# A recommendation tower on one core: ten tables looked up on TensorE in pairs, with loads of 112 + 13 partitions, rings for rows and pairs, and five parts

## The reference, cut to what matters

```python
e = jnp.stack([tbl_0[ids[:, 0]], ..., tbl_25[ids[:, 25]]], axis=1)      # 512 x 26 x 128
all_emb = jnp.concatenate([bottom_output[:, None, :], e], axis=1)       # 512 x 27 x 128
gram = jnp.einsum('bfd,bgd->bfg', all_emb, all_emb)
z = gram[:, _TRIU_I, _TRIU_J]                                           # 512 x 351
h = jnp.concatenate([z, r_bottom_output], axis=1)
h = jnp.maximum(h @ W_top1 + b_top1, 0.0)                               # 512 x 512
h = jnp.maximum(h @ W_top2 + b_top2, 0.0)                               # 512 x 256
y = h @ W_top3                                                          # 512 x 1
```

## Time and profile before

| | |
|---|---|
| three runs | 166.47, 171.18, 188.59 (median 171.18) |
| the profiled execution, from first to last instruction | 164.9 |
| TensorE busy with matmuls | 111.2 (67%), 700 records |
| GpSimd busy | 79.3 (48%), 72 gathers among it |
| VectorE, ScalarE busy | 60.0 (36%), 54.4 (33%) |
| HBM read, written | 13.70 MB, 1.49 MB |
| mean granted TensorE clock | 0.845 of full |

### The profile page before, as it was taken

How to read it: one execution, slowest core, us unless ns; L and a number is a source line. 1 busy time by engine, 2 the same in 40 slices (tenths; PEclk the granted TensorE clock), 3 DMA queues, 4 the chain that set the end, 5 groups by cost and what they waited for, 6 DMA issues and landing times.

```text
span 164.9 us, 1891 instructions
## 1 busy us (share of the span) xinstructions
PE 111.2 (67%) x700; PEld 97.8 (59%) x700; DVE 60.0 (36%) x109; ACT 54.4 (33%) x78; POOL 79.3 (48%) x81
## 2 busy tenths in 40 slices
PE   6809949968734968935300006259999999999784
PEld 6707737746624746925200006139999989979583
DVE  1046956965808494202000020042364442531110
ACT  3051963574627192202000020043354433342011
POOL 4277877887778787777777777100000000010200
PEclk9975896999997899996955555555899999999999
DMA  2954554566546942212212211106114152006100
GB/s 52 247 159 162 180 186 156 178 188 191 169 158 191 227 137 79 61 48 50 62 48 48 63 49 48 32 0 90 44 28 74 36 79 43 16 0 93 48 0 0
DMA packets 19501, 15.32 MB, mean 93 GB/s; under 512 B 13764, under 2 KB 15680, under 8 KB 19492
## 3 DMA queue, kind: packets, MB, share of 16 engines
q1 hardware_dynamic: 14562, 10.06, 22.3%
q0 software_dynamic: 2416, 4.82, 11.6%
q10 hardware_dynamic: 2514, 0.32, 1.3%
HBM read 13.70 MB, written 1.49 MB: 92 GB/s over the span
## 4 chain that ended last, share of the span: by engine, by line
PE 36%; DMA 30%; issue 18%; DVE 5%; ACT 4%; another core or an unknown queue 3%; SPq 2%; ACTq 1%; DVEq 0%
PE banks L460 19%; DMA lookup_ids_sb<-in_lookup_ids 14%; DMA raw<-in_tbl 13%; PE banks L498 5%; PE banks L441 4%; DVE low L646 3%; PE banks L505 3%; DMA products_dram<-products 2%; PE banks L424 2%; ACT products L598 2%; PE banks L426 2%; DVE one_hot L632 2%; ACTq L323 1%; DMA pairs<-products_dram 1%
## 5 line engine op out<-in xcount | busy, mean ns | idle before, releaser
L358 POOL DMA_INDIRECT mixed_sb<-in_mixed_table,mixed_rows_sb x64 | 67.8, 1059 | 22.1 <-issue 19.2
L460 PE MATMUL banks<-turned 128*112 128x104 f32 x256 | 34.1, 292 | 30.7 <-issue 25.3
L460 PEld LDWEIGHTS banks<-turned 128*112 128x112 f32 x256 | 31.8, 206 | 32.1 <-issue 30.6
L424 PE MATMUL banks<-one_hot,high 125*128 125x512 f32 x60 | 27.6, 459 | 16.7 <-DVE low L646 14.3
L598 DVE COPY products<-banks 112x416 f32<-112x416 f32 (+2 forms) x17 | 14.0, 839 | 57.3 <-PE banks L460 29.5
L598 ACT COPY products<-banks 112x416 f32<-112x416 f32 (+2 forms) x17 | 14.1, 843 | 57.7 <-PE banks L460 29.9
L632 DVE TENSOR_SCALAR one_hot<-lookup_ids_sb,starts_sb 125x512 fp32r<-125x512 int32 x60 | 26.6, 490 | 18.0 <-DMA lookup_ids_sb<-in_lookup_ids 12.8
L426 PE MATMUL banks<-one_hot,low 125*128 125x512 f32 x60 | 26.6, 444 | 0.0
L424 PEld LDWEIGHTS banks<-one_hot,high 125*128 125x128 f32 x60 | 13.4, 223 | 21.7 <-issue 18.5
L323 POOL DMA_DIRECT2D products_dram<-products x1 | 0.8, 846 | 44.0 <-DVE products L598 44.0
L683 ACT CAST high<-raw 125x1024 fp32r<-125x1024 f32 (+1 forms) x8 | 8.8, 1101 | 29.0 <-DMA raw<-in_tbl 29.0
(11 more groups left out here) (32 smaller groups left out, 75.1 us busy)
## 6 DMA issues: line engine op xcount, KB each, us to landing
raw<-in_tbl SPq DMA_DIRECT2D x6, 500.0 KB
lookup_ids_sb<-in_lookup_ids SPq DMA_DIRECT2D x8, 256.0 KB, 8.7
raw<-in_tbl SPq DMA_DIRECT2D x2, 625.0 KB
products_dram<-products SPq DMA_DIRECT2D x12, 91.0 KB
mixed_sb<-in_mixed_table,mixed_rows_sb POOLq DMA_INDIRECT x64
pairs<-products_dram SPq DMA_DIRECT2D x16, 39.0 KB
w_sb<-in_w SPq DMA_DIRECT2D x2, 256.0 KB
w_sb<-in_w SPq DMA_DIRECT2D x1, 512.0 KB
```

Of the source, the lines that this page charges most:

```text
L358: pool.indirect_dma_start(mixed_sb[:, n, :], None, mixed_table, bass.IndirectOffsetOnAxis(ap=mixed_rows_sb[:, n:n + 1], axis=0),).then_inc ...
L424: pe.matmul(lookup_ps[:, i % 2, :], high[0:TABLE_PARTS, i % 2, c, :], columns, start=(c == 0), stop=False)
L460: last = pe.matmul(product_ps[0:QUAD * SLOTS, b % 2, k // half, k % half, 0:QUAD * OTHERS], turned[:, t, q, :, :].rearrange("p j f -> p (j ...
```

## The change

- Ten tables are looked up on TensorE (six of 1,000 rows, four of 1,250), and no side gathers are left. The two tables join the lookups; the mixed table has the same 16 tables.
- Two tables of the same size form a duo. Their ids stand side by side, so that one instruction makes the one-hot matrices of both (125 x 1,024). TensorE does chunk 0 of the first, chunk 0 of the second, chunk 1 of the first and so on, four matmuls a chunk. A duo has two banks; the six banks 2 to 7 serve three duos. ScalarE's one-hot is now made in place.
- A table is loaded by two DMAs, 112 partitions and 13, in place of one with 125.
- `high` and `low` are rings of 4 tables, `lookup_ids_sb` of 2 duos, the one-hot ring has 3. `mixed_sb` is a ring of 32 gathers: gather n waits until block (n - 32)/4 is turned. `pairs` is a ring of two parts; the load of part p waits until layer 1 of part p - 2 is done.
- The ids of the mixed gathers are loaded by SP as its first DMA, so that `starts` is ScalarE's first.
- The last two blocks have 2 and 2 gathers. There are five parts: blocks 0-3, 4-7, 8-11, 12-14 and 15-16 (128, 128, 128, 96 and 32 samples). The outputs of three parts are woven in, by a new `LATE_ORDER`.

```diff
-PARTS = [(0, 4), (4, 8), (8, 12), (12, 17)]
-EARLY_PARTS = 2
+PARTS = [(0, 4), (4, 8), (8, 12), (12, 15), (15, 17)]
+EARLY_PARTS = 3
-LATE_ORDER = "ot m ot m oo m to to m oo to m o to m t o t m m oo"
+TURNS_AFTER = [0, 1, 2, 1, 2]
+LATE_ORDER = ("m t m t m t m t m t m m m m"
+              " oooo to oto m m m oooo to oo m m oooo tm tm tm ooo")
...
+            if p >= 2:
+
+                eng.wait_ge(layer_done, (p - 2) * OUTS + OUTS1)
             eng.wait_ge(stored[p], 16 * len(hardware_stores(p)))
...
+            for b in range(BLOCKS):
+                for n in range(FIRST_GATHER[b], FIRST_GATHER[b + 1]):
+                    if n >= MIXED_RING:
+                        pool.wait_ge(group_turned, block_of(n - MIXED_RING) + 1)
...
-                sp.dma_start(raw[0:TABLE_PARTS, i % RAW_RING, 0:CHUNKS_OF[i], :].rearrange("p c d -> p (c d)"),
-                             lookup_tables[i].rearrange("(p c) d -> p (c d)", p=TABLE_PARTS)
-                             ).then_inc(table_in[i], 16)
+                for first, end in ((0, WIDE_PARTS), (WIDE_PARTS, TABLE_PARTS)):
+                    sp.dma_start(raw[first:end, i % RAW_RING, 0:chunks, :].rearrange("p c d -> p (c d)"),
+                                 table[first:end, :]).then_inc(table_in[i], 16)
...
+            def make_one_hots(d):
+                dve.wait_ge(lookup_ids_in[d], 16)
+                make_one_hot(d, 0)
+                make_low(PAIRED * d)
+                make_one_hot(d, 1)
+                make_low(PAIRED * d + 1)
+                for c in range(2, VECTOR_CHUNKS_OF[d]):
+                    make_one_hot(d, c)
...
             for step, n in PLAN:
                 if step == "lookup":
                     copy_lookup(n)
-                    if n + 2 < len(LOOKUP):
-                        round_table(n + 2)
+                    if n + 2 < DUOS:
+                        for i in range(PAIRED * (n + 2), PAIRED * (n + 3)):
+                            round_table(i)
                         make_one_hots(n + 2)
```

319 lines of the change are left out of this document (142 added, 177 removed).

## The result

| | before | after |
|---|---|---|
| times of the executions, us | 166.5, 171.2, 186.2, 188.6 | 176.6, 177.4, 177.9, 178.0 |
| profiled execution, its span | 164.9 | 176.1 |
| lookups end | 64.8 | 60.8 |
| last gather starts | 102.9 | 96.4 |
| block 3's `keep` starts | 109.3 | 101.6 and 102.2 |

The change made the kernel slower: 1.062 times the time before, 95% interval 1.056 to 1.068. That ratio compares undisturbed executions alone; the kernel before has longer ones too (186 and 189), so that the two medians, 178.7 and 177.7, look alike. The prediction was 157.0.

The account below looks back on a forecast made before the run. Table transfers pace the lookups, TensorE is then held until the gathers end, and afterwards TensorE is the bound. TensorE free at 96.8, plus 58.6 to the end, plus 1.6 around it gave 157.0 us; range 120 to 168.

Parts of the forecast that it names:

- First gather 3.5: Start of the mixed gathers: with `starts` first in ScalarE's queue, the first gather at 3.5 us in place of 8.22.
- Table loads: In the lookups: split loads use more DMA engines, an estimated 1.9 us a table instead of 6.06.
- The rule against splitting: Table loads: transfers to disjoint partitions serialise, so the split gives no speed; in the slower rival, 175 us, chance 0.10.
- VectorE, one-hots of 0.71: In the lookups: a one-hot of 1,024 columns takes 0.71 us, or 0.89 if it were twice the work.
- Lookups end at 56: End of the lookups: start 10, matmuls 40.0, slow first stretch 2.5, lost at duos 3.5; bounds 53 to 62.
- Last gather 91: End of the gathers: 36 at 1.47 us until the lookups end, then 28 at 1.25; range 89 to 95.
- The stretch ends with the gathers: Late stretch: TensorE is free 5.5 us after the gathers end at 91, at 96.8; chance 0.50.
- gone: Rival for the late stretch: TensorE's delay after the lookups does not come back, 123 us; chance 0.20.
- From there to the end 58.6: From TensorE free to the end: 55.6 before, less 2.2 for turns, plus 2.9 for a fifth part, plus 2.3 waits.
- Waits of 2.3: Last stage: waits for the pairs of parts 2 and 3 cost some 2.3 us more together than before.
- `pairs` as a ring costs nothing: Last stage: load 2 waits for part 0's layer 1, which stands before block 9, so no cost.
- Slower, 0.12: Whole kernel over 2% slower, chance 0.12; its rival: ring stops gathers, last lookup from 86 on, 175 us.

Follow-up runs that it names:

- e3: The kernel before with each table loaded as 112 + 13 partitions instead of one load of 125: 167.0 us (163.1 to 168.7).
- e4: The changed kernel with the split undone, each table one load of 125 partitions: 185.7 us, ratio 1.110 to the kernel before.
- e2: The changed kernel with only 36 of its 64 gathers issued, so part of the result is wrong: 155.8 us (141.9 to 171.3).
- e11: The changed kernel with four parts, part 2's outputs behind the last block, run a second time: 160.8 us, ratio 0.937 to the kernel before.
- e9: The changed kernel without any edit, run again beside the kernel before: 176.7 us against 188.2.
- f1: The changed kernel with 8 unused matmuls of 512 columns before each of TensorE's last two waits for pairs: 175.1 us (167.4 to 181.6).
- f2: The changed kernel without any edit, as control on its chip: 183.5 us (177.9 to 187.0).
- f3: The changed kernel with four parts but its order kept, part 2's outputs before the last blocks: 169.8 us (169.1 to 175.7).
- e12: The kernel before with split loads, `starts` and mixed ids first, and first mixed gathers ahead of side gathers: 165.0 us, ratio 0.969.
- f4: The changed kernel with four parts and a matmul of 512 columns before each product of blocks 1 to 6: 166.6 us (165.2 to 175.4).
- g1: The changed kernel with four parts, GpSimd waiting before five gathers until given blocks are reported multiplied: 158.9 us; kernel before beside it 169.6.
- g2: The kernel before with split loads and early first gather, GpSimd waiting before seven gathers for blocks reported multiplied: 160.2 us, ratio 0.884.
- e5: The changed kernel with an unused matmul of 512 columns before each product of blocks 0 to 8: 163.0 us; kernel before beside it 130.4.
- e8: The changed kernel with 16 unused matmuls of 512 columns before each of TensorE's last two waits for pairs: 147.0 us, ratio 1.135.
- e6: The changed kernel with an awaited small memset on GpSimd behind each gather from number 36 on: 145.7 us (140.2 to 148.9).

## Why the prediction was wrong, step by step

The miss is 177.9 - 157.0 = 20.9 us: 4.1 until TensorE is free (100.9 instead of 96.8), 16.6 from there to the end (75.2 instead of 58.6), 0.2 around it. The step that failed is the second: the sum for the last stage took +2.9 for a fifth part, and it and the order that came with it cost 16.7.

- **First gather 3.5**: right (3.47).
- **Table loads**: right. Split alone (e3) and undone (e4) show it from both sides. The estimate of 1.9 us a table was not reached (3.3 to 4.3 in e3); the changed kernel's DMA engines were 0.92 busy from 12 to 36 at 244 GB/s, so little was left to gain. The rule against splitting, which made one of the rivals, comes with a reason that does not fit this load, as told under e3.
- **VectorE, one-hots of 0.71**: 0.76. **Lookups end at 56**: 60.8, inside the bounds of 53 to 62. The start was 11.1 instead of 10: the second table came late (ScalarE waited 4.3 us for it before its rounding at 11.23, with the DMA engines 1.04 busy by the profile's count from 8 to 12), which also cost TensorE 1.5 at 13.76. From its first matmul to 60.8 TensorE is idle for 4.1 in all, against 3.5 in the sum. Four groups of turns stand between the lookups, 1.8 at 0.44 each, and were in no term. The 11 MB in 44 us "just enough" should have been a term for the start, not a remark.
- **Last gather 91**: 96.4, outside my range. Gathers in the lookups were 1.61 apart instead of 1.47 (first to 33rd: 3.5 to 54.9), 4.5 us over 32 of them, and the ring stopped GpSimd for 1.7 at 92.7. The prediction priced the ring only for lookups that end beyond 86, though it listed a gather that waits for it as a sign of being wrong; it costs a little whenever TensorE's report of a turn is late.
- **The stretch ends with the gathers**: right (e2, e3). TensorE was free 3.6 us behind the end of the last gather (97.4 to 100.9) against 5.5 predicted, so that 1.9 of luck hid a part of the gathers' 6.0: together the 4.1. Against its absence (the rival "gone", 0.20) the prediction had that "all three runs before have it", which says nothing of other chips. On one of five chips the kernel before took 130 and none of the four kernels was held. There "gone" (123) is the true case. The changed kernel with fillers took 147 even there; that the term below is the reason is argued, since four parts were not run on that chip.
- **From there to the end 58.6**: this step failed, and in it one term: "A fifth part ... at 96 and 32 columns together I take +2.9". The control for it is e11: four parts need 58.1 (98.4 to 156.5), five 74.8 (e9: 99.7 to 174.5). The 16.7 are, by the last `keep` of each (139.5 and 146.1): 5.3 in front of it, since part 2's outputs no longer fill the wait for the last pairs but stand before the last blocks; and 11.4 behind it, of which the clock is 9.3 (f1, f2) and what is left 2.1. f3 changes the number of parts alone and parts the 16.7 another way: it needs 66.2 (107.7 to 173.9), 9.4 less than its control f2 (100.5 to 176.1) and 8.1 more than e11 (on another chip), so that about half is the fifth part and half the new place of part 2's outputs, each with its share of the clock. The prediction had no term for the clock and none for that place. The part's matmuls were not cheaper for having fewer columns: 24 records of 128, 96 and 32 columns took 2.84, 2.81 and 2.76 at the full clock. I had 5.6 for full width (the rows give 5.4) and discounted it without a row to say so.
- **Waits of 2.3**: near. From 110 to 150 TensorE stood idle for 4.5 us against 0.8, 3.7 more. They are not the fifth part's: e11 has 3.7 from 103 to 143. Four parts with these waits would have been 55.6 - 2.2 + 2.3 = 55.7 by the prediction and took 58.1; 2.4 of the miss are there.
- **`pairs` as a ring costs nothing**: no run isolates it; no load in the trace waited for it that I could find.
- **Slower, 0.12**: I tied slower to a last lookup at 86. e4 is that case (94.1, 185 to 195). The change was slower for something no rival named: the last stage, and in it above all TensorE's clock. The waits before the last parts were priced as idle time alone, not by what the engine does after them.

## What to carry to other kernels

Cutting the last stage finer pays only if the pieces are cheaper and the clock stays full: price small matmuls at full width unless a row shows otherwise, and look what the granted clock does behind each wait that a cut makes. Work that fills the last wait is worth its place; moving part 2's outputs ahead of the last blocks cost 5.3 us there and left TensorE idle before the pairs.

Where an engine's work is reported long after it was taken on, look for what streams beside it, and for pauses of that stream; a stage that ends with the stream takes back most of what is won before it. And run the kernel before on more than one chip before tying a forecast to a stretch that no instruction explains.

## What the runs showed of the hardware

- The hold. While GpSimd's gathers follow each other, the reports of TensorE's work can come late, by up to 50 us (e3: 55.3 to 105.2). The profile shows instructions of TensorE then 0.7 us or a multiple apart:

```profile
99.45 0.33 PE L414 MATMUL banks<-turned 128*112 128x104 f32 x1 [0.37 <-issue]
100.15 0.37 PE L397 MATMUL banks<-identity,mixed_sb 128*128 128x128 f32 x1 [0.37 <-issue]
100.85 0.37 PE L397 MATMUL banks<-identity,mixed_sb 128*128 128x128 f32 x1 [0.33 <-issue]
```

  It ends up to 9 us behind the start of the last gather before a pause (e2 0.3, f3 1.6, e4 4.1, after 4.5, e3 4.9, e11 5.5, e12 9.0). Single reports also come before any pause (after 84.0, before 98.0, e12 99.7). It comes beside products and, in some executions, beside lookups (e2, e4, f1, f3, f4, g1, g2). I take the 182 to 193 us executions of the kernel before for such a hold in its lookups, where its gathers never pause; none was profiled, so that is argued, not shown. What starts it, and the path on which it happens, stay open, and so does whether TensorE finished its work late or only its report was late.
- It came on four of the five chips of the groups; on the other one the kernel before took 128.4 to 134.1 instead of 164 to 193, and no profile there (e5 to e8) shows it.
- The granted clock fell to 0.5, the lower of its two levels (1.2 of 2.4 GHz), at 154 to 155 in the changed kernel, after 149 to 154 in which TensorE was busy for 2.3 of 5 us, and stayed there for over 20 us of which TensorE worked 20.07 of 22. With eight matmuls of 512 columns in each wait it was full until the last layer (f1), and in e6 it was full for most of that stage without them.
- A record of 32 columns in layer 1 takes 0.115 us at the full clock (f1) and 0.22 at the low one (f2), one of 128 columns 0.118 (e11).
